# Spreading a block-maximum pass evenly over four attention stages of a fused attention + channel-mix layer, on 8 cores

## The reference

```
xn = layernorm(x)                                   # x: [16, 2048, 1024]
out = x + attn(xn) + ffn(xn)
attn, per batch and head (32 pairs on a core), blocks of 32 tokens, n = 64 blocks:
  low   = mean(Q blocks) @ mean(K blocks).T * 0.125         # 64 x 64
  norm  = low - rowmax(low) + 5000 on the diagonal band
  hi_mask = norm >= the 1024th largest of norm
  hi    = Q K^T * 0.125 for the selected blocks only
  max_vals[row] = max of hi over the selected blocks of this row
  hi_out, hi_norm = exp(hi - max_vals) V, row sums
  low_attn = exp(low - rowmax - 1e4*hi_mask) * 32   -> low_out, low_norm
  out = (hi_out*hi_corr + low_out*low_corr) / (hi_norm*hi_corr + low_norm*low_corr + 1e-6)
ffn: r = sigmoid(xr Wr^T); k = relu(xk Wk^T)^2; r * (k Wv^T)
```

## Time and profile before

| what | value |
|---|---|
| median of 3 runs | 6459.17 us (6459.16 to 6503.45) |
| the profiled execution | 6461.08 us, of which span of the slowest core 6459.5 us |
| spans of the eight cores | 6430.1 to 6459.5 us |
| mean granted TensorE clock | 0.676 to 0.679 of full speed |
| PE busy | 3597.1 us (56%) |
| DVE (VectorE) busy | 2505.6 us (39%) |
| ACT (ScalarE) busy | 1708.6 us (26%) |
| loop over p | 8 turns of some 518 us each |

### The profile page before, as it was taken

The page is one execution under the profiler, slowest core; times in us unless marked ns, Lnnn a source line. Parts: engine busy times, 40 slices in busy tenths (PEclk is TensorE's granted clock), DMA queues, the critical chain, the costliest instruction groups (busy, mean ns, idle before and its releaser), DMA issues.

```text
span 6459.5 us, 53953 instructions; the slowest of 8 cores (6430.1 to 6459.5 us)
## 1 busy us (share of the span) xinstructions
PE 3597.1 (56%) x11513; PEld 1157.3 (18%) x11513; DVE 2505.6 (39%) x5263; ACT 1708.6 (26%) x2627; POOL 213.0 (3%) x269
## 2 busy tenths in 40 slices
PE   1121023333333357767777777776776776777676
PEld 0021011111111111122121222122112112112121
DVE  3512134443343224515415434533542451542543
ACT  2200000000000013343342442343334334334244
POOL 0000100000000000000000000000000000000000
PEclk9955566677767766676675666666567667667566
DMA  1242012222222211001101101001001100111010
GB/s 61 59 87 57 3 30 61 59 61 65 65 62 65 65 36 24 14 20 28 24 18 24 30 14 28 17 20 35 17 14 31 27 14 20 25 27 25 12 27 14
DMA packets 523421, 223.42 MB, mean 35 GB/s; under 512 B 494794, under 2 KB 495986, under 8 KB 522930
## 3 DMA queue, kind: packets, MB, share of 16 engines
q1 hardware_dynamic: 486994, 155.63, 10.1%
q0 software_dynamic: 36128, 64.34, 4.2%
HBM read 167.40 MB, written 47.73 MB: 33 GB/s over the span
## 4 chain that ended last, share of the span: by engine, by line
PE 36%; DVE 23%; DMA 19%; issue 11%; ACT 9%; DVEq 1%; ACTq 0%; POOL 0%; SPq 0%; POOLq 0%
DVE bm L769 11%; PE pO L804 9%; PE pA L761 8%; PE pS L836 8%; PE pA L995 4%; ACT aT L856 3%; DMA fW<-wT_r 2%; PE pA L516 2%; DMA fW<-wT_k 2%; DMA fW<-wT_v 2%; DMA bx<-bsm_dram 2%; ACT stage L934 2%; DMA nb<-norm_all 2%; DVE fA L501 2%; DMA xtile<-x 1%
## 5 line engine op out<-in xcount | busy, mean ns | idle before, releaser
L769 DVE TENSOR_REDUCE bm<-pA 128x16 f32<-128x512 f32 x2048 | 1416.7, 692 | 1421.8 <-PE pA L761 1256.7
L856 ACT ACTIVATE aT<-pS 128x1024 bf16<-128x1024 f32 x1024 | 1048.6, 1024 | 1343.4 <-PE pS L836 1291.0
L761 PE MATMUL pA<-ktp,qtp 64*128 64x512 bf16 x2048 | 1031.6, 545 | 588.8 <-DVE bm L769 400.2
L804 PE MATMUL pO<-aT,vtm 128*65 128x512 bf16 x2048 | 865.0, 516 | 377.2 <-ACT aT L856 367.8
L836 PE MATMUL pS<-rhsc,lhsc 128*128 128x512 bf16 x2048 | 863.3, 519 | 29.1 <-DVE rhsc L724 29.1
L516 PE MATMUL pA<-fA,fW 128*128 128x512 bf16 x1536 | 417.6, 424 | 287.9 <-DMA fW<-wT_r 72.1
L761 PEld LDWEIGHTS pA<-ktp,qtp 64*128 64x128 bf16 x2048 | 176.8, 101 | 1471.6 <-issue 1468.7
L804 PEld LDWEIGHTS pO<-aT,vtm 128*65 128x65 bf16 x2048 | 265.7, 144 | 857.1 <-issue 825.6
L417 PE MATMUL pB<-bis_cnt,ones 128*128 128x32 f32 x116 | 35.1, 397 | 684.4 <-DVE bis_cnt L413 684.4
L836 PEld LDWEIGHTS pS<-rhsc,lhsc 128*128 128x128 bf16 x2048 | 180.1, 113 | 411.0 <-issue 362.1
L516 PEld LDWEIGHTS pA<-fA,fW 128*128 128x128 bf16 x1536 | 152.2, 106 | 547.6 <-issue 438.5
(11 more groups left out here) (144 smaller groups left out, 2429.0 us busy)
## 6 DMA issues: line engine op xcount, KB each, us to landing
xtile<-x SPq DMA_DIRECT2D x64, 512.0 KB
xtile<-part_sc SPq DMA_DIRECT2D x64, 512.0 KB
fW<-wT_r SPq DMA_DIRECT2D x64, 256.0 KB
fW<-wT_k SPq DMA_DIRECT2D x64, 256.0 KB
fW<-wT_v SPq DMA_DIRECT2D x64, 256.0 KB
bx<-bsm_dram POOLq DMA_DIRECT2D x32, 512.0 KB, 8.3
out<-stage SPq DMA_DIRECT2D x32, 512.0 KB
part_sc<-ptile POOLq DMA_DIRECT2D x16, 512.0 KB, 3.0
```

The lines of the kernel that those rows point to most:

```text
L761: e.matmul(pA[:, half * 512:(half + 1) * 512], qtp[p0:p0 + 64, ts0 + t * 128:ts0 + (t + 1) * 128], ktp[p0:p0 + 64, ts0 + kq * 512:ts0 + (k ...
L769: nred = r.emit("vector", lambda e, kq=kq, half=half: e.tensor_reduce(bm[:, kq * 16:(kq + 1) * 16], pA[:, half * 512:(half + 1) * 512] .re ...
L804: e.matmul(pO[:, sl * 512:(sl + 1) * 512], vtm[:, (sq * 16 + k) * 130 + hip * 65: (sq * 16 + k) * 130 + hip * 65 + 65], aT[bpar][:, sl * 5 ...
L856: e.activation(aT[bpar][:, :], pS[bpar][:, :], AF.Exp, scale=0.125))
```

## The change

The 192 units of stages 1, 2 and 3 are spread by two a kg, and stage 3 takes a share:

| in stage | kg | units of |
|---|---|---|
| 0 | 0 to 31 | stage 1: 0 to 63 |
| 1 | 8 to 31 | stage 2: 0 to 47 |
| 2 | 8 to 15 | stage 2: 48 to 63 (its own) |
| 2 | 16 to 31 | stage 3: 0 to 31 |
| 3 | 8 to 23 | stage 3: 32 to 63 (its own) |

The loads of `bx` and `rmb` move into a function of their own, `emit_prep_bx`. For stage 1 it is called in `emit_prep` as before, for stage 2 at kg 0 of stage 1, for stage 3 at kg 16 of stage 2. The wait for `phA_done_dv` goes with it. The two waits of a unit on the epilogue's use of `pA` (`pA_free_ac`, `ndv_ep`) now stand ahead of every unit, not only of units 0 and 1.

```diff
--- before.py
+++ after.py
@@ -696,16 +696,9 @@
                      "pcons": [0, 0], "nac_qk": 0, "nsy_part": [0, 0], "ngp_add": [0, 0],
                      "nst_a2": [0, 0], "pA_free_ac": [0, 0], "pending_w1": None}
 
-            def emit_prep(p, hip, sq, par, prev_chunk_pe):
+            def emit_prep_bx(p, hip, sq):
                 b = bh_idx(p, hip, sq)
-                p0 = 64 * hip
-                ts0 = sq * S
-                r.wait("gpsimd", "sPE", prev_chunk_pe)
                 r.wait("gpsimd", "sDV", state["phA_done_dv"])
-                r.emit("gpsimd", lambda e, p0=p0, ts0=ts0, par=par: e.dma_start(
-                    rhs2[par][0:64, :], qtp[p0:p0 + 64, ts0:ts0 + S]))
-                r.emit("gpsimd", lambda e, p0=p0, ts0=ts0, par=par: e.dma_start(
-                    lhs2[par][0:64, :], ktp[p0:p0 + 64, ts0:ts0 + S]))
                 state["ngp_bx"] = r.emit("gpsimd", lambda e, b=b: e.dma_start(
                     bx[:, :],
                     bsm_dram[b].rearrange("j t k -> j (t k)")
@@ -713,6 +706,18 @@
                 state["ngp_rmb"] = r.emit("gpsimd", lambda e, b=b: e.dma_start(
                     rmb[:, :],
                     rm_dram[b].unsqueeze(1).broadcast_to([4, 32, 16])))
+
+            def emit_prep(p, hip, sq, par, prev_chunk_pe, with_bx=False):
+                b = bh_idx(p, hip, sq)
+                p0 = 64 * hip
+                ts0 = sq * S
+                r.wait("gpsimd", "sPE", prev_chunk_pe)
+                r.emit("gpsimd", lambda e, p0=p0, ts0=ts0, par=par: e.dma_start(
+                    rhs2[par][0:64, :], qtp[p0:p0 + 64, ts0:ts0 + S]))
+                r.emit("gpsimd", lambda e, p0=p0, ts0=ts0, par=par: e.dma_start(
+                    lhs2[par][0:64, :], ktp[p0:p0 + 64, ts0:ts0 + S]))
+                if with_bx:
+                    emit_prep_bx(p, hip, sq)
                 h = 2 * p + hip
                 r.wait("sync", "sGC", state["ngp_add"][par])
                 state["nsy_part"][par] = r.emit(
@@ -751,9 +756,8 @@
                 half = u % 2
                 r.wait("tensor", "sDV", state["phA_dv2"][half])
                 r.wait("tensor", "sAC", state["pcons"][half])
-                if u < 2:
-                    r.wait("tensor", "sAC", state["pA_free_ac"][half])
-                    r.wait("tensor", "sDV", state["ndv_ep"])
+                r.wait("tensor", "sAC", state["pA_free_ac"][half])
+                r.wait("tensor", "sDV", state["ndv_ep"])
                 if u == 0:
                     r.wait("tensor", "sGP", state["ngp_bx"])
                     r.wait("tensor", "sAC", state["nac_qk"])
@@ -824,7 +828,7 @@
                                                     outT[:, qh * 1024:(qh + 1) * 1024],
                                                     pO[:, :], AF.Copy))
 
-            def emit_chunk_iter(p, hip, sq, par, kg, nxt):
+            def emit_chunk_iter(p, hip, sq, par, kg, units):
                 qh, k = kg // 16, kg % 16
                 kpar = kg % 2
                 r.wait("tensor", "sAC", state["prev_exp"][kpar])
@@ -844,13 +848,8 @@
                 if kg == 4 and state["pending_w1"] is not None:
                     state["pending_w1"]()
                     state["pending_w1"] = None
-                if nxt is not None and kg >= 8:
-                    if kg < 24:
-                        us = range((kg - 8) * 3, (kg - 8) * 3 + 3)
-                    else:
-                        us = range(48 + (kg - 24) * 2, 48 + (kg - 24) * 2 + 2)
-                    for u in us:
-                        emit_phaseA_half(*nxt, u)
+                for bhu, u in units:
+                    emit_phaseA_half(*bhu, u)
                 r.wait("scalar", "sPE", npe_s)
                 newexp = r.emit("scalar", lambda e, bpar=kpar:
                                 e.activation(aT[bpar][:, :], pS[bpar][:, :],
@@ -1006,7 +1005,7 @@
                 bhs = [(p, hip, sq) for hip in range(2) for sq in range(B_CORE)]
                 state["nac_qk"] = r.cnt["sAC"]
                 r.wait("gpsimd", "sAC", r.cnt["sAC"])
-                emit_prep(*bhs[0], 0, 0)
+                emit_prep(*bhs[0], 0, 0, with_bx=True)
                 vsl = [(pS[0], 0), (pS[0], 512), (pS[1], 0), (pS[1], 512)]
                 vcons = [0] * 4
                 u_phA = 0
@@ -1072,10 +1071,32 @@
                 for i in range(4):
                     par = i % 2
                     if i < 3:
-                        emit_prep(*bhs[i + 1], (i + 1) % 2, state["chunk_pe_end"])
+                        emit_prep(*bhs[i + 1], (i + 1) % 2, state["chunk_pe_end"],
+                                  with_bx=(i == 0))
                     for kg in range(32):
-                        emit_chunk_iter(*bhs[i], par, kg,
-                                        bhs[i + 1] if i < 3 else None)
+                        units = []
+                        if i == 0:
+                            units = [(bhs[1], 2 * kg), (bhs[1], 2 * kg + 1)]
+                        elif i == 1:
+                            if kg == 0:
+                                emit_prep_bx(*bhs[2])
+                            if kg >= 8:
+                                u0 = 2 * (kg - 8)
+                                units = [(bhs[2], u0), (bhs[2], u0 + 1)]
+                        elif i == 2:
+                            if kg == 16:
+                                emit_prep_bx(*bhs[3])
+                            if 8 <= kg < 16:
+                                u0 = 48 + 2 * (kg - 8)
+                                units = [(bhs[2], u0), (bhs[2], u0 + 1)]
+                            elif kg >= 16:
+                                u0 = 2 * (kg - 16)
+                                units = [(bhs[3], u0), (bhs[3], u0 + 1)]
+                        else:
+                            if 8 <= kg < 24:
+                                u0 = 32 + 2 * (kg - 8)
+                                units = [(bhs[3], u0), (bhs[3], u0 + 1)]
+                        emit_chunk_iter(*bhs[i], par, kg, units)
                     emit_av(*bhs[i], par, 31)
                     state["chunk_pe_end"] = r.cnt["sPE"]
                     emit_epilogue(*bhs[i], par, i == 3)
```

## The result

The changed kernel takes 6058.9 us (median of 10 runs, 6048.6 to 6097.5) against 6465.8 (median of 10, 6459.2 to 6503.5). The ratio is 0.937, 95% interval 0.935 to 0.939: 6.3% faster. Forecast were 6046 and a range of 5985 to 6220. The profiled execution has a span of 6056.6 us on its slowest core, core 7, 402.9 less than before.

What follows compares the result with a forecast made beforehand. TensorE and VectorE waiting in turn, with TensorE's low clock, bound the kernel. Per turn -16.2 - 34.3 - 21.9 + 16.1 + 4.4 = -51.9 us; eight turns, -415, from 6461.1 give 6046, range 5985 to 6220.

Steps and rivals of the forecast that it cites:

- What bounds: Phase A: TensorE and VectorE wait for each other in turn; a kg costs 4.06 us with three units, 1.915 with two.
- The clock stays up with two units a kg: Two-unit kg: TensorE's clock rises to 1.00 after one to five kg and does not fall before the units end.
- Rivals 1 and 2: Two-unit kg at clock 0.50: all of them, 6711 us, chance 0.08; or half of them, 6379 us, chance 0.12.
- Starts at the low clock: Each new stretch of units runs 2.5 kg at 2.79 instead of 1.915 us: +2.2 us.
- 1.915 us a kg: Kg with two units at full clock: VectorE sets the pace without a gap, 3.83 us for two kg.
- The added waits: Two more TensorE waits ahead of each unit, some 0.03 us each: 4.4 us a turn, 14.6 if nothing is covered.
- Rival 3: Added waits stand on the path of release, matmul and next reduction: 10.2 us more a turn, 6127 us, chance 0.18.
- Stage 0 behind `bx`: Unit 0 waits for the load of `bx`, about 15 us on TensorE; the stage takes 89.1 us, -16.2.
- Stage 2: New load of `bx` exposed after unit 63, 11.6 us, TensorE waiting 9 to 11; the stage takes 87.4 us, -21.9.
- ScalarE's order behind unit 63: TensorE waits 3.9 us for the exponential behind unit 63; gone from two stage ends, now at kg 15 and kg 23.
- Stage 3: Kg 8 to 23 now hold units: 38.6 us against 22.5, +16.1.
- The sum: All parts give -51.9 us a turn, -415 in eight turns, from 6461.1 to 6046 us.

Runs made afterwards that it cites:

- units between: Kernel before, but a kg's three units stand apart (ahead of the scores, between scores and values, behind the values); 6266.7 us, ratio 0.970.
- Three and one: Changed kernel with the same units in the same pairs of kg, three in the even kg and one in the odd; 6439.7 us, ratio 0.997.
- second buffer: Changed kernel with a second buffer for `bx` and a second `rmb`, each load issued one phase A earlier; 5885.0 us, ratio 0.912.
- last run: Added to second buffer, few waits and next turn's first `bx` loaded early: ScalarE's exponential of unit 63 behind the next scores exponential; 5644.5 us, ratio 0.876.
- few waits: Changed kernel with the two added waits only where an epilogue may still use `pA`, not ahead of every unit; 5991.8 us, ratio 0.928.
- two `bx` with few waits: Changed kernel with the edits of second buffer and few waits together; 5812.0 us, ratio 0.900.

## Why the prediction was right, point by point

- **What bounds.** Right: two engines in turn, and the clock. The runs separate what I had priced as one number, 4.06. At the low clock the third unit's wait is 0.59 us a kg (units between), and without it three units still take 3.47; with the wait but at the higher clock, a kg of three took 2.78.
- **The clock stays up with two units a kg.** Right in the main: 655 of 768 kg at full clock. Rivals 1 and 2 did not come. Three and one shows that they were no straw men: the same mean came to 0.50 in long pieces. But the clock did fall once in 18 of 24 stages, behind the change of halves, and the sum has no term for that.
- **Starts at the low clock.** Too dear where a stretch begins at kg 8: I took 2.5 kg, some 7 us at 0.50, and in stages 1, 2 and 3 it was 1.6 us at most. This and the falls that I had left out have opposite signs.
- **1.915 us a kg.** Too low by 0.06 in the changed kernel (3.95 for two). Exactly right once the waits are few (3.83).
- **The added waits.** The term that failed. I took 0.03 us a wait and 4.4 us a turn, with 14.6 as the far end. Measured: 0.105 a wait where a release is on the path, 7.5 (turn) to 8.4 us (67 / 8) a turn. The step that was wrong is that VectorE's 3.83 covers them: it has a gap in every two kg. Rival 3 had the right mechanism, a ring with little to spare, and was partly true. In the value transposes the price of 0.03 was right and the count was not: I charged one unit of each pair, +2.1, and both pay, 84.9 to 88.9, +4.0.
- **Stage 0 behind `bx`.** Right: the wait is 14.78, the stage 90.6 for 89.1, and the second buffer took it away.
- **Stage 2.** The interval was right, 11.2 us for 11.6, the stage 85.7 for 87.4. What the profile would show of it was wrong: I named 9 to 11 us of waiting for `bx` on TensorE, and it is 5.39, since 3.26 of the interval goes to the late exponential and the rest to matmuls. So the waits for `bx` in stages 0 and 2 sum to 163 us, not to 200; the page's 248 holds 85 us of the value transposes besides, which were there before (83) and which I had left out.
- **ScalarE's order behind unit 63.** Right, by the last run: 4.1 to 5.2 us at each of three places a turn.
- **Stage 3.** +16.1 was forecast, and +2.1 behind it; measured +22.1 for both. The trace splits it: +17.4 in stage 3, +4.0 in the value transposes, +0.7 in the projections between, which the change does not touch.
- **The sum.** 6046 against 6059. The misses a turn are +1.5, +1.0, -1.7 and +3.9 by the rows of the table; the 2.3 us of waits that the sum held besides cover half of their total. That it comes within 13 us is in part luck: without the 4.4 us of added waits the sum would have been 6011, and the kernel with few waits took 5992. So the rest of the forecast was some 20 us too high, and the waits some 30 us too low.

## What to carry to other kernels

When two engines hand a small buffer to and fro, count what a step costs with one, two or three pieces before moving them: here, at the lower clock, a kg took 1.70 us without units (kg 7 of a stage 1, 3594.93 to 3596.63), 2.79 with two and 4.06 with three, so the third cost more than the first two. The even distribution also let TensorE's clock rise, and with it a kg of two took 1.98. Ask what the clock does at every place where the pattern is broken, and not only inside it. A wait that is always met is not free if it stands behind the wait that is met last; put a guard only where the buffer changes hands. When work is moved earlier, its loads must move too: the change left 20 us a turn exposed behind a single-buffered load, and a second buffer brought another four tenths of what the change had brought.

## What the runs showed that I had not expected

- A wait on TensorE cost 0.105 us behind a late release and about 0.03 behind running matmuls.
- TensorE busy 40.04 of 41 us with three units a kg ran at a clock of 0.50 throughout, while with two units a kg, busy 19.77 of 24 us, it ran at 1.00.
- In some executions a granted clock between the two levels appeared. With few waits the profiled core had it in stage 1 of seven turns of eight, for 13 to 21 us around the change of halves; in the turn below it began at 3467.7 and ended at 3489.0:

```profile
3480.00:3489.00 9.00, 6.66 (x25) 1.79 (x22) 5.67 (x11) 5.12 (x5) 0.00 (x0) 0.81 0.00 0
3491.00:3505.00 14.00, 11.92 (x45) 3.78 (x44) 11.84 (x22) 7.47 (x8) 0.00 (x0) 1.00 0.00 0
```

Most kg in it took some 1.8 and 2.1 to 2.2 us in turn, where 1.6 and 2.2 came at 1.00. It was not the few waits that brought it: in the profiled execution two `bx` with few waits had it on no core, and units between, with its waits as before, had it for 200 us in all on the profiled core. No run here was made to find what grants 0.81.
